# A graph-network kernel: messages of the last two aggregations in two float32r parts instead of three bf16 parts, with the cast of the counts shared by ScalarE and VectorE

## The chip, the cores and the metric

One core of a Trainium2 chip. The metric is the device time in microseconds (us) of one launch; lower is better. The chip multiplies on TensorE (PE in the profile's rows, PEld for its weight loads), and works element by element on VectorE (DVE), ScalarE (ACT) and GpSimd (POOL). SyncE (SP) issues most of the DMAs.

## What is computed

Four graph layers over 1875 nodes with 256 features and 60000 edges, each followed by a residual add and a layer norm. The change is in the third layer, which applies this convolution twice, with the same edges both times:

```python
def _sage_conv(x, src, dst, W_proj, b_proj, W_l, b_l, W_r):
    xp = jax.nn.relu(x @ W_proj + b_proj)
    msg_sum = jax.ops.segment_sum(xp[src], dst, num_segments=n)
    cnt = jax.ops.segment_sum(jnp.ones_like(dst, dtype=x.dtype), dst, num_segments=n)
    aggr = msg_sum / jnp.maximum(cnt, 1.0)[:, None]
    out = aggr @ W_l + b_l + x @ W_r
    norm = jnp.linalg.norm(out, axis=-1, keepdims=True)
    return out / jnp.maximum(norm, EPS)
```

`msg_sum` is what this text calls an aggregation: for each destination node, the sum of the rows `xp` of its sources.

## The kernel before, in words

**The counts.** In its long first part the kernel walks over the edges and builds the array `ADJ`: for each source node and each destination node the number of edges between them, as 16-bit integers. A partition holds one source of each tile of 128; the free dimension runs over 1888 destinations (`NW`) and, innermost, over 15 tiles of sources (`SH`, the same number as `NT`). One "chunk" of counts is what one tile of sources needs: 1888 elements, read at a stride of 15 elements.

**An aggregation** (`aggregate`, lines 1739 to 1757) is then a dense product. For each of the 15 chunks TensorE multiplies the messages of a source tile (128 by 256, the stationary operand, in two halves of 128 features) with the chunk (the moving operand, four pieces of 472 columns, `CW`), and adds in all eight PSUM banks. The messages are float32 values; to keep their precision they are held as a sum of three bf16 parts (hi, mid, lo), so a chunk costs 3 x 2 x 4 = 24 matmuls. The chunk is float16, which holds the small counts exactly. There are two chunk buffers: `chunk(at, c % 2, wide)`. ScalarE casts chunk c (`cast2`, lines 719 to 723, called from `messages2`) once TensorE has used chunk c - 2 (semaphore `chunk_used`), and TensorE waits for it (`chunk_ready`). Chunks 0 and 1 are cast early (`early_cast`): for the first convolution in the stage of the layer before, for the second during the output stage of the first. Two loops exist of everything, for small and for large counts (`wide`); with these inputs the small-count one runs. In the second layer there is a similar aggregation over 30 chunks (`CH1`), which the change leaves as it is.

**Messages.** Before an aggregation, `project` (line 1800) makes each tile of `x @ W_proj + b_proj` in one of four banks: one bf16 matmul for the bias and two float32 matmuls. ScalarE writes the relu of it as bf16 (`message`, line 678: hi). VectorE computes the rest from the bank: `rest` (line 1268), three dependent instructions: the remainder (line 1274), its bf16 cast (line 1275, mid), and the difference (line 1276, lo), after which `p_ev` lets TensorE use the bank again. TensorE starts the aggregation when all 15 tiles are through (line 1827).

**After an aggregation** VectorE and ScalarE copy the eight banks out (`agg_evac`, lines 1297 and 715). The output stage follows: for each of 15 tiles, float32 matmuls with `W_l` (line 1836) and `W_r` (line 1839), and the scaling, the norm and the relu on VectorE and ScalarE. In the first convolution the result is transposed on TensorE (line 1696) for the second.

**The order of the work** is written by hand, engine by engine. Every engine runs the loop `for u in range(2)` over the two convolutions: TensorE at line 1823, ScalarE at 753 (as v), VectorE at 1358. In the second one VectorE also runs `attention_columns` (line 1345): eight instructions on the weights of the fourth layer (lines 1350 and 1351). They stand between the last message and the copy of the banks. They wait for three DMAs (`ld_wt3`) that SyncE issues when the output stage of the first convolution is through TensorE.

Of the kernel before, what the change touches and what calls it, by code (L numbers as in the profile page):

```python
# [21 lines left out]
F32 = mybir.dt.float32  # L22
F16 = mybir.dt.float16
BF16 = mybir.dt.bfloat16
I32 = mybir.dt.int32
SP, DVE, PE = mybir.EngineType.SP, mybir.EngineType.DVE, mybir.EngineType.PE
U16 = mybir.dt.uint16
# [6 lines left out]
D = 256  # L34
P = 128
# [132 lines left out]
def build(nc, rec, x, xT, edge0, w0, a0l, a0r, cols, hrow, wrel, brow, wih, w1, w2, w3, b3, wp1, bp1, wl1, bl1, wr1, wp2, bp2, wl2, bl2, wr2,  # L168
          wt3, a3l, a3r, out):
    ctx = ExitStack()  # L170
    with ctx:
# [8 lines left out]
        sorted_t = nc.dram_tensor("sorted_records", (EP, 4), I32).ap()  # L180
        al_t = nc.dram_tensor("al_table", (NP, H), F32).ap()

        AR = sb("arena", [P, A_END], F32)
        ADJ = sb("adjacency", [P, R2, NW * SH], U16)
        ident = sb("ident", [P, P], F32)
# [119 lines left out]
        def parts(i):  # L305
            return [MT[i].bitcast(BF16)[:, D * q:D * (q + 1)] for q in range(3)]

        WIDE = [AR[:, A_B1 + D * i:A_B1 + D * (i + 1)] for i in range(R2 * NT)]

        def chunk(at, k, wide):  # L310

            if wide:
                return AR[:, at[1] + k * NW:at[1] + (k + 1) * NW]
            return AR[:, at[0] + k * NW // 2:at[0] + (k + 1) * NW // 2].bitcast(F16)
# [27 lines left out]
            feat_ev diag_done bc_mm sel_free collected cmp_done ws_mm selr_ready djr_mm sel_ready fld_mm fld_ev steps_done a_oh a_mm a_ev a_add  # L342
            pool_link lane_mm lane_ev flags_in flags_mm tail_ready tail_mm cin_ready cin_mm exp_ready exp_done
            alpha_ready als_mm als_ev r_oh r_wgt r_mm ld_hb ld_x ld_bc ld_wt1 ht_ready ht_add
            var_ready std_ready ln_done xt_mm xt_eva xt_evd h_mm h_ev m_mm m_ev chunk_ready chunk_used agg_eva
            agg_evd gate_mm gate_ev c_ready tc_ready hn_ready x1_mm x1_ev x2_mm x2_ev x3_mm x3_add ld_b2 ld_wt2 ld_wt3
            p_mm p_ev hi_ready cnt_red cnt_mm big_mm o_mm o_ready nrm_done h_ready pool_gate vl3_done t_mm t_ev t_st key_mm
            key_ev er_st er_ld erw_ready kc_ev oht er_mm er_red et_mm et_ev selt sc_mm flag_cmp flag_mm
# [213 lines left out]
        def _(act):  # L562
# [112 lines left out]
                    xt_evac(0, q - 1)  # L675
            xt_evac(0, 3)

            def message(n, bank, wide):

                dst = WIDE[n % (R2 * NT)] if wide else parts(n % (R2 * NT))[0]  # L680
                a.activation(dst, PS[bank][:, 0:D], ACT.Relu).then_inc(s["hi_ready"], 1)

            def messages1(wide):
# [35 lines left out]
            def cast2(v, c, wide):  # L719
                if c >= 2:  # L720
                    act.wait_ge(s["chunk_used"], (R2 + v) * SH + c - 1)
                a.activation(chunk(CH2, c % 2, wide), ADJ[:, 0, :].rearrange("p (n s) -> p n s", s=SH)[:, :, c],  # L722
                             ACT.Copy).then_inc(s["chunk_ready"], 1)

            def early_cast(v, c):
# [27 lines left out]
            for v in range(2):  # L753
                def messages2(wide):
                    for t in range(NT):
                        act.wait_ge(s["p_mm"], NT * v + t + 1)
                        message(t, t % 4, wide)
                    for c in range(2, SH):
                        cast2(v, c, wide)

                with act.If(large < 1):
                    messages2(False)
                with act.If(large >= 1):
                    messages2(True)
                agg_evac(B2T, (R2 + 1 + v) * SH)
                if v == 0:
                    early_cast(1, 0)
                    early_cast(1, 1)
                for q, (t0, t1) in enumerate(GROUPS):
                    act.wait_ge(s["o_ready"], NT * v + t1)  # L770
                    a.activation(RS[:, t0:t1], RS[:, t0:t1], ACT.Sqrt).then_inc(s["nrm_done"], 1)
                    if v == 0 and q:
                        xt_evac(2, q - 1)
                    if v == 1:
                        ln_sqrt(7 + q, t0, t1)
                    if v == 1 and q >= 2:
                        xt_evac(3, q - 2)
                if v == 0:
                    xt_evac(2, 3)
# [14 lines left out]
        def _(dve):  # L794
# [473 lines left out]
            def rest(n, slot, bank, done, before):  # L1268
# [6 lines left out]
                link(v.tensor_copy(mid, REM))  # L1275
                v.tensor_tensor(lo, REM, mid, ALU.subtract).then_inc(done, 1)  # L1276

            def no_rest(n, done):

                dve.wait_ge(s["hi_ready"], n + 1)  # L1280
                dve.sem_inc(s["dve_link"], 2)
                dve.sem_inc(done, 1)
# [62 lines left out]
            def attention_columns():  # L1345

                dve.wait_ge(s["ld_wt3"], 48)
                for lr in range(2):
                    for k in range(2):
# [5 lines left out]
                        else:  # L1355
                            link(ins)

            for u in range(2):
                with dve.If(large < 1):
                    for t in range(NT):  # L1360
                        rest(R2 * NT + u * NT + t, t, t % 4, s["p_ev"], u * NT + t)
                chain[0] -= 2 * NT
                with dve.If(large >= 1):
                    for t in range(NT):
                        no_rest(R2 * NT + u * NT + t, s["p_ev"])
                chain[0] += 2 * NT
                if u == 1:
                    attention_columns()
                agg_evac(B2T, base + (u + 1) * SH)
                for q, (t0, t1) in enumerate(GROUPS):  # L1370
                    for t in range(t0, t1):
                        dve.wait_ge(s["o_mm"], NT * u + t + 1)
                        link(v.tensor_scalar(B1[:, t, :], PS[t % 4][:, 0:D], RC[:, t:t + 1], None, ALU.mult))
                        link(v.tensor_tensor(B1[:, t, :], B1[:, t, :], PS[t % 4][:, D:2 * D], ALU.add))
                        v.tensor_tensor_reduce(out=REM, in0=B1[:, t, :], in1=B1[:, t, :], scale=1.0, scalar=0.0,
                                               op0=ALU.mult, op1=ALU.add, accum_out=RS[:, t:t + 1]).then_inc(s["o_ready"], 1)
                    if u == 1 and q:
                        normalise(6 + q, *GROUPS[q - 1])
                    dve.wait_ge(s["nrm_done"], 4 * u + q + 1)
                    link(v.tensor_scalar(RS[:, t0:t1], RS[:, t0:t1], 1e-12, None, ALU.max))  # L1380
                    link(v.reciprocal(RS[:, t0:t1], RS[:, t0:t1]))
                    for t in range(t0, t1):
                        if u == 0:
                            ins = v.tensor_scalar(B1[:, t, :], B1[:, t, :], RS[:, t:t + 1], 0.0, ALU.mult, ALU.max)
                        else:
                            ins = v.scalar_tensor_tensor(X[:, t, :], B1[:, t, :], RS[:, t:t + 1], X[:, t, :], ALU.mult, ALU.add)
                    if u == 0:
                        ins.then_inc(s["h_ready"], 1)
                        if q:
                            xt_evac(2, q - 1)  # L1390
                    else:
                        link(ins)
                        link(stats(t0, t1))
                        variance(t0, t1)
                        if q >= 2:
                            xt_evac(3, q - 2)
                if u == 0:
                    xt_evac(2, 3)
# [44 lines left out]
        def _(pe):  # L1443
# [295 lines left out]
            def aggregate(at, n, first):  # L1739


                def products(wide):
                    for c in range(n):
                        pe.wait_ge(s["chunk_ready"], first + c + 1)
                        ch = chunk(at, c % 2, wide)
                        ms = [WIDE[c]] if wide else parts(c)
                        for q, m in enumerate(ms):
                            for fo in range(2):
                                for j in range(4):
# [161 lines left out]
```

## Time and profile before

| | us |
|---|---|
| three runs of the kernel | 1827.79, 1826.61, 1823.5 |
| median | 1826.61 |
| span of the profiled execution, first to last instruction | 1946.7 |
| PE, DVE, ACT busy in it | 1461.8, 1153.3, 786.8 |
| first aggregation of the third layer, in the trace | 1599.1 to 1671.0 |
| second one | 1735.1 to 1809.8 |

For the profiled execution only its span is known, and it stands 120.1 us above the median of the runs that were timed without a profile. In the rows, `L1750` is line 1750 of the kernel before; a line such as "1599.13 71.87 PE L1750 ... x360" gives the start of a group of instructions, its length and how many they are. The count of matmuls for a float32 operand is twice that in the code: each is recorded as two instructions. A granted clock (PEclk) of 1.00 is TensorE's full 2.4 GHz; its lower level is 1.2 GHz.

### The profile page before, as it was taken

To read this page: it belongs to the slowest core of one execution; us is meant where nothing else is said; L and a number is where in the kernel's file an instruction comes from. 1 tells how busy PE (TensorE), PEld (TensorE's weight loads), DVE (VectorE), ACT (ScalarE), POOL (GpSimd) and SP (SyncE) were. 2 spreads that over 40 slices of the span, in tenths; PEclk is the share of its full clock that TensorE was granted. 3 is DMA by queue.
4 is the path that set the end of the run, shared out by engine and by line. 5 is a ranking of instruction groups with operands and counts; after the bars stand their busy time and mean duration, and the time that the engine had idled before them with its cause. 6 is when DMAs were issued, how large, how long until landed. Compare 5 with 4: busy or idle time off the path is not lost.

```text
span 1946.7 us, 22362 instructions
## 1 busy us (share of the span) xinstructions
PE 1461.8 (75%) x5398; PEld 733.7 (38%) x5398; DVE 1153.3 (59%) x3024; ACT 786.8 (40%) x1243; POOL 531.3 (27%) x517
## 2 busy tenths in 40 slices
PE   5894765577666766666359999798999889989930
PEld 3342433231111111111237777554445444644620
DVE  5412432239888988898999999852181460450636
ACT  1331332237666766676200000035774527327121
POOL 0105555556757666775000000000000000000023
PEclk9996555575555555555559999899999989999975
DMA  3535455554545455554129888300000010000022
GB/s 149 166 141 170 143 164 166 173 162 142 177 150 177 150 166 170 173 172 151 44 84 307 270 271 269 96 1 24 1 1 1 0 33 1 1 11 1 1 61 63
DMA packets 84509, 223.94 MB, mean 115 GB/s; under 512 B 18456, under 2 KB 27588, under 8 KB 83908
## 3 DMA queue, kind: packets, MB, share of 16 engines
q1 hardware_dynamic: 60452, 158.01, 23.4%
q0 software_dynamic: 23968, 64.77, 12.6%
q8 instruction: 53, 0.87, 0.2%
q14 instruction: 36, 0.29, 0.0%
HBM read 140.09 MB, written 82.63 MB: 114 GB/s over the span
## 4 chain that ended last, share of the span: by engine, by line
PE 38%; DVE 15%; issue 6%; DVEq 2%; ACT 1%; DMA 1%; POOL 0%; another core or an unknown queue 0%; SPq 0%; POOLq 0%
PE bank L1750 15%; PE bank L1687 11%; PE bank L1770 2%; DVE arena L1126 2%; DVE arena L1084 2%; PE bank L1734 2%; DVE adjacency L1091 2%; PE bank L1709 1%; DVE arena L1085 1%; PE bank L1839 1%; PE bank L1836 1%; PE bank L1816 1%; DVE arena L1276 1%; DVE arena L1274 1%; DVE arena L1172 1%
## 5 line engine op out<-in xcount | busy, mean ns | idle before, releaser
L547 POOL DMA_INDIRECT arena<-feat_table,arena x469 | 494.5, 1054 | 365.6 <-issue 231.4
L1626 PE MATMUL bank<-arena 128*128 128x480 f16 x586 | 337.2, 577 | 165.9 <-DVE arena L1085 96.7
L629 ACT ACTIVATE arena<-bank 128x480 uint16<-128x480 f32 x586 | 332.6, 572 | 164.4 <-PE bank L1626 109.4
L1750 PE MATMUL bank<-arena 128*128 128x472 f16 x1440 | 291.4, 366 | 10.5 <-DVE arena L1276 6.5
L555 POOL DMA_INDIRECT arena<-al_table,edge_ends x15 | 14.3, 956 | 964.7 <-DMA al_table<-arena 960.4
L1091 DVE TENSOR_TENSOR adjacency<-adjacency,arena 128x480 uint16 x586 | 234.3, 400 | 38.8 <-issue 22.8
L1687 PE MATMUL bank<-arena 128*128 x966 | 229.5, 392 | 0.8 <-issue 0.3
L1626 PEld LDWEIGHTS bank<-arena 128*128 128x128 f16 x586 | 60.9, 104 | 442.4 <-issue 219.9
L1750 PEld LDWEIGHTS bank<-arena 128*128 128x128 bf16 x1440 | 141.8, 99 | 160.2 <-issue 12.4
L1085 DVE TENSOR_SCALAR arena<-iota,arena 128x480 f16<-128x480 f16 x586 | 199.0, 340 | 0.0
L1687 PEld LDWEIGHTS bank<-arena 128*128 128x128 f32 x966 | 174.0, 190 | 56.6 <-issue 35.3
L1182 DVE TENSOR_TENSOR arena<-arena 128x1024 f32<-128x1024 f32 x118 | 140.3, 1213 | 16.9 <-DMA arena<-edge_rows 15.2
L1084 DVE TENSOR_SCALAR arena<-iota,arena 128x128 f16<-128x128 f16 x586 | 145.4, 248 | 4.1 <-ACT adjacency L593 4.1
L722 ACT ACTIVATE arena<-adjacency 128x1888 f16<-128x1888 uint16 x30 | 108.8, 3633 | 45.9 <-PE bank L1750 45.9
L703 ACT ACTIVATE arena<-adjacency 128x1888 f16<-128x1888 uint16 x30 | 109.0, 3636 | 33.7 <-PE bank L1750 33.7
L1589 PE MATMUL bank<-arena 128*128 x588 | 75.9, 187 | 53.3 <-issue 47.7
L1546 PE MATMUL bank<-arena 128*128 128x512 f32 x240 | 111.4, 620 | 5.9 <-ACT arena L578 3.0
L605 ACT ACTIVATE arena<-bank 128x512 f16<-128x512 f32 x64 | 35.3, 597 | 173.6 <-remote 81.1
L1575 PE MATMUL bank<-adjacency,ident 128*128 128x512 f16 x128 | 67.4, 617 | 47.1 <-DVE arena L1041 35.5
L661 ACT ACT_TABLE_LOAD x2 | 2.6, 1283 | 239.8 <-DVE ln_mean_var L1228 239.8
L1297 DVE COPY arena<-bank 128x472 f32<-128x472 f32 x12 | 7.0, 642 | 143.4 <-PE bank L1750 143.3
L1589 PEld LDWEIGHTS bank<-arena 128*128 128x128 f16 x588 | 58.6, 105 | 86.4 <-issue 74.7
(289 smaller groups left out, 1544.6 us busy)
## 6 DMA issues: line engine op xcount, KB each, us to landing
arena<-edge_rows SPq DMA_DIRECT2D x117, 520.0 KB, 4.7
edge_rows<-arena SPq DMA_DIRECT2D x67, 520.0 KB
edge_rows<-arena SPq DMA_DIRECT2D x67, 390.0 KB
feat_table<-arena SPq DMA_DIRECT2D x60, 260.0 KB, 2.1
arena<-feat_table,arena POOLq DMA_INDIRECT x469
arena<-in_w SPq DMA_DIRECT2D x1, 2048.0 KB, 10.1
arena<-in_xT SPq DMA_DIRECT2D x1, 1920.0 KB, 18.3
arena<-in_x SPq DMA_DIRECT2D x1, 1792.0 KB
```

What stands on the lines that cost most here:

```text
L547: g.indirect_dma_start(out=PLACE[k][:, t - lo, :], out_offset=None, in_=feat_t, in_offset=bass.IndirectOffsetOnAxis(ap=IE[:, t:t + 1], axi ...
L629: a.activation(EV[st % AS].rearrange("p r k -> p (r k)"), PS[4 + st % 4][:, 0:R2 * KW], ACT.Copy)\
L703: a.activation(chunk(CH1, c % 2, wide), ADJ[:, r, :].rearrange("p (n s) -> p n s", s=SH)[:, :, sh], ACT.Copy).then_inc(s["chunk_ready"], 1)
L1084: v.tensor_scalar(OHS[st % AS], iota128[:, :], lo, None, ALU.is_equal)
L1085: v.tensor_scalar(OHK[st % AS], iota480[:, :], key, None, ALU.is_equal).then_inc(s["a_oh"], 1)
L1091: v.tensor_tensor(dst, dst, EV[st % AS], ALU.add).then_inc(s["a_add"], 1)
L1182: v.tensor_tensor(rows, rows, al, ALU.mult).then_inc(s["r_wgt"], 1)
L1546: ins = mm(PS[c][:, :], XT0[:, k, P * t:P * (t + 1)], W0[:, k, 512 * c:512 * (c + 1)], start=(k == 0), stop=(k == 1))
L1589: ins = mm(PS[4 + g % 2][:, 3 * H * k:3 * H * (k + 1)], KO[g % 3][:, lo:lo + P], ERW[:, bass.ds(offs[k], 3 * H)], start=True, stop=True)
L1626: mm(PS[4 + st % 4][:, 0:R2 * KW], OHS[st % AS], OHK[st % AS], start=True, stop=True).then_inc(s["a_mm"], 1)
L1687: mm(BANKS[:, bass.ds(out_at, D)], OHR[:, (st // RG) % ORING, P * (st % RG):P * (st % RG + 1)], FBf[:, bass.ds(places[st % RK] >> 12, D)], ...
L1750: ins = mm(PS[4 * fo + j][:, 0:CW], m[:, P * fo:P * (fo + 1)], ch[:, CW * j:CW * (j + 1)], start=(c == 0 and q == 0), stop=(c == n - 1 and ...
```

## The change

Only the two aggregations of the third layer change (`CH2`).

- A message is held as two parts of type float32r, hi and lo, in a new view of the same memory (`halves`, `HALVES`). ScalarE writes hi; VectorE writes lo in one instruction (`low_half`) instead of the three of `rest`. 
- A chunk is float32r too (`COUNTS`). A chunk costs 2 x 2 x 4 = 16 matmuls instead of 24. Both operands of each are now float32r.
- From chunk 2 on ScalarE casts the first 944 destinations of a chunk and VectorE the other 944 (`second_halves`), after a wait of its own for `chunk_used`; a new semaphore `chunk_half` adds a second wait to TensorE's. ScalarE still casts chunks 0 and 1 whole.
- In the second convolution `attention_columns` moves on VectorE ahead of the messages.

```diff
--- before.py
+++ after.py
@@ -22,6 +22,7 @@
 F32 = mybir.dt.float32
 F16 = mybir.dt.float16
 BF16 = mybir.dt.bfloat16
+F32R = mybir.dt.float32r
 I32 = mybir.dt.int32
 SP, DVE, PE = mybir.EngineType.SP, mybir.EngineType.DVE, mybir.EngineType.PE
 U16 = mybir.dt.uint16
@@ -180,6 +181,7 @@
         sorted_t = nc.dram_tensor("sorted_records", (EP, 4), I32).ap()
         al_t = nc.dram_tensor("al_table", (NP, H), F32).ap()
 
+        a_at = -(-nc.sbuf_base // 32) * 32
         AR = sb("arena", [P, A_END], F32)
         ADJ = sb("adjacency", [P, R2, NW * SH], U16)
         ident = sb("ident", [P, P], F32)
@@ -305,10 +307,18 @@
         def parts(i):
             return [MT[i].bitcast(BF16)[:, D * q:D * (q + 1)] for q in range(3)]
 
+        HALVES = nc.alloc_sbuf_tensor_at("message_halves", [P, 2 * NT * D], F32R, offset=a_at + 4 * A_B1)
+        COUNTS = nc.alloc_sbuf_tensor_at("count_chunks", [P, 2 * NW], F32R, offset=a_at + 4 * A_CH)
+
+        def halves(i):
+            return [HALVES[:, D * (2 * i + q):D * (2 * i + q + 1)] for q in range(2)]
+
         WIDE = [AR[:, A_B1 + D * i:A_B1 + D * (i + 1)] for i in range(R2 * NT)]
 
         def chunk(at, k, wide):
 
+            if at == CH2 and not wide:
+                return COUNTS[:, k * NW:(k + 1) * NW]
             if wide:
                 return AR[:, at[1] + k * NW:at[1] + (k + 1) * NW]
             return AR[:, at[0] + k * NW // 2:at[0] + (k + 1) * NW // 2].bitcast(F16)
@@ -342,7 +352,7 @@
             feat_ev diag_done bc_mm sel_free collected cmp_done ws_mm selr_ready djr_mm sel_ready fld_mm fld_ev steps_done a_oh a_mm a_ev a_add
             pool_link lane_mm lane_ev flags_in flags_mm tail_ready tail_mm cin_ready cin_mm exp_ready exp_done
             alpha_ready als_mm als_ev r_oh r_wgt r_mm ld_hb ld_x ld_bc ld_wt1 ht_ready ht_add
-            var_ready std_ready ln_done xt_mm xt_eva xt_evd h_mm h_ev m_mm m_ev chunk_ready chunk_used agg_eva
+            var_ready std_ready ln_done xt_mm xt_eva xt_evd h_mm h_ev m_mm m_ev chunk_ready chunk_half chunk_used agg_eva
             agg_evd gate_mm gate_ev c_ready tc_ready hn_ready x1_mm x1_ev x2_mm x2_ev x3_mm x3_add ld_b2 ld_wt2 ld_wt3
             p_mm p_ev hi_ready cnt_red cnt_mm big_mm o_mm o_ready nrm_done h_ready pool_gate vl3_done t_mm t_ev t_st key_mm
             key_ev er_st er_ld erw_ready kc_ev oht er_mm er_red et_mm et_ev selt sc_mm flag_cmp flag_mm
@@ -675,9 +685,9 @@
                     xt_evac(0, q - 1)
             xt_evac(0, 3)
 
-            def message(n, bank, wide):
-
-                dst = WIDE[n % (R2 * NT)] if wide else parts(n % (R2 * NT))[0]
+            def message(n, bank, wide, exact=False):
+
+                dst = WIDE[n % (R2 * NT)] if wide else halves(n)[0] if exact else parts(n % (R2 * NT))[0]
                 a.activation(dst, PS[bank][:, 0:D], ACT.Relu).then_inc(s["hi_ready"], 1)
 
             def messages1(wide):
@@ -719,7 +729,8 @@
             def cast2(v, c, wide):
                 if c >= 2:
                     act.wait_ge(s["chunk_used"], (R2 + v) * SH + c - 1)
-                a.activation(chunk(CH2, c % 2, wide), ADJ[:, 0, :].rearrange("p (n s) -> p n s", s=SH)[:, :, c],
+                n = NW if c < 2 else NW // 2
+                a.activation(chunk(CH2, c % 2, wide)[:, 0:n], ADJ[:, 0, :].rearrange("p (n s) -> p n s", s=SH)[:, 0:n, c],
                              ACT.Copy).then_inc(s["chunk_ready"], 1)
 
             def early_cast(v, c):
@@ -754,7 +765,7 @@
                 def messages2(wide):
                     for t in range(NT):
                         act.wait_ge(s["p_mm"], NT * v + t + 1)
-                        message(t, t % 4, wide)
+                        message(t, t % 4, wide, True)
                     for c in range(2, SH):
                         cast2(v, c, wide)
 
@@ -1274,6 +1285,12 @@
                 link(v.scalar_tensor_tensor(REM, PS[bank][:, 0:D], 0.0, hi, ALU.max, ALU.subtract))
                 link(v.tensor_copy(mid, REM))
                 v.tensor_tensor(lo, REM, mid, ALU.subtract).then_inc(done, 1)
+
+            def low_half(n, slot, bank, done):
+
+                hi, lo = halves(slot)
+                dve.wait_ge(s["hi_ready"], n + 1)
+                v.scalar_tensor_tensor(lo, PS[bank][:, 0:D], 0.0, hi, ALU.max, ALU.subtract).then_inc(done, 1)
 
             def no_rest(n, done):
 
@@ -1355,17 +1372,24 @@
                         else:
                             link(ins)
 
+            def second_halves(u, wide):
+                for c in range(2, SH):
+                    dve.wait_ge(s["chunk_used"], (R2 + u) * SH + c - 1)
+                    v.tensor_copy(chunk(CH2, c % 2, wide)[:, NW // 2:NW], ADJ[:, 0, :].rearrange("p (n s) -> p n s", s=SH)[:, NW // 2:NW, c])\
+                     .then_inc(s["chunk_half"], 1)
+
             for u in range(2):
+                if u == 1:
+                    attention_columns()
                 with dve.If(large < 1):
                     for t in range(NT):
-                        rest(R2 * NT + u * NT + t, t, t % 4, s["p_ev"], u * NT + t)
-                chain[0] -= 2 * NT
+                        low_half(R2 * NT + u * NT + t, t, t % 4, s["p_ev"])
+                    second_halves(u, False)
                 with dve.If(large >= 1):
                     for t in range(NT):
-                        no_rest(R2 * NT + u * NT + t, s["p_ev"])
-                chain[0] += 2 * NT
-                if u == 1:
-                    attention_columns()
+                        dve.wait_ge(s["hi_ready"], R2 * NT + u * NT + t + 1)
+                        dve.sem_inc(s["p_ev"], 1)
+                    second_halves(u, True)
                 agg_evac(B2T, base + (u + 1) * SH)
                 for q, (t0, t1) in enumerate(GROUPS):
                     for t in range(t0, t1):
@@ -1742,8 +1766,10 @@
                 def products(wide):
                     for c in range(n):
                         pe.wait_ge(s["chunk_ready"], first + c + 1)
+                        if at == CH2 and c >= 2:
+                            pe.wait_ge(s["chunk_half"], (first // SH - R2) * (SH - 2) + c - 1)
                         ch = chunk(at, c % 2, wide)
-                        ms = [WIDE[c]] if wide else parts(c)
+                        ms = [WIDE[c]] if wide else halves(c) if at == CH2 else parts(c)
                         for q, m in enumerate(ms):
                             for fo in range(2):
                                 for j in range(4):
```

## Rows read from the trace of the kernel before

**Rows 1.** Windows: length, busy time by engine, granted clock, DMA share, GB/s.
```profile
1599.10:1671.00 71.90, 71.87 (x360) 35.14 (x360) 0.00 (x0) 47.19 (x13) 0.00 (x0) 1.00 0.00 1
...
1735.10:1809.80 74.70, 74.59 (x360) 35.89 (x360) 3.19 (x9) 47.23 (x14) 0.00 (x0) 0.96 0.00 1
```

**Rows 2.** Timeline, first aggregation: start, length, instruction, idle before.
```profile
1604.12 3.63 ACT L722 ACTIVATE arena<-adjacency 128x1888 f16<-128x1888 uint16 x1 [7.05 <-PE bank L1750]
1608.90 3.62 ACT L722 ACTIVATE arena<-adjacency 128x1888 f16<-128x1888 uint16 x1 [1.15 <-PE bank L1750]
...
1599.13 71.87 PE L1750 MATMUL bank<-arena 128*128 128x472 f16 x360 [2.48 <-DVE arena L1276]
```

**Rows 3.** Chain of waits in the first output stage: start, length, piece.
```profile
1675.88 0.86 PE bank L1836 x4
...
1690.83 0.87 PE bank L1696 x8
```

**Rows 4.** Groups by form: busy us, mean ns; float32 weight loads.
```profile
L1836 PEld LDWEIGHTS bank<-arena 128*128 128x128 f32 x120 | 22.8, 193 | 9.2 <-DVE arena L1298 5.9 <-DVE ln_rstd L1375 0.4
```

**Rows 5.** Groups by form: a ScalarE copy to float16; VectorE reads.
```profile
L605 ACT ACTIVATE arena<-bank 128x512 f16<-128x512 f32 x64 | 35.3, 597 | 173.6 <-remote 81.1 <-PE bank L1577 50.9 <-PE bank L1575 28.7
...
L1302 DVE TENSOR_REDUCE arena<-adjacency 128x1888 f32<-128x28320 uint16 x1 | 29.7, 29653 | 0.0
...
L1422 DVE TENSOR_REDUCE arena<-arena 128x64 f32<-128x256 f32 x15 | 7.8, 576 | 0.1
```

**Rows 6.** Timeline: end of the first convolution's messages.
```profile
1595.52 1.13 PE L1807 MATMUL bank<-arena 128*128 128x256 f32 x4
...
1596.69 0.38 ACT L681 ACTIVATE arena<-bank 128x256 bf16<-128x256 f32 x1 [0.89 <-PE bank L1807]
...
1598.53 0.43 DVE L1276 TENSOR_TENSOR arena<-arena 128x256 bf16<-128x256 f32 x1
```

**Rows 7.** Timeline: the second convolution's messages.
```profile
1710.50 1.13 PE L1807 MATMUL bank<-arena 128*128 128x256 f32 x4
...
1711.77 1.13 PE L1807 MATMUL bank<-arena 128*128 128x256 f32 x4
...
1714.01 0.82 PE L1696 MATMUL bank<-ident,arena 128*128 128x128 f32 x6
...
1714.87 0.56 DVE L1242 COPY arena<-bank 128x384 f32<-128x384 f32 x1 [3.74 <-PE bank L1696]
...
1716.61 0.28 PE L1805 MATMUL bank<-arena,ones 3*128 3x256 bf16 x1 [1.78 <-DVE arena L1276]
...
1728.45 0.28 PE L1805 MATMUL bank<-arena,ones 3*128 3x256 bf16 x1
...
1729.77 0.28 PE L1805 MATMUL bank<-arena,ones 3*128 3x256 bf16 x1
...
1729.98 1.13 PE L1807 MATMUL bank<-arena 128*128 128x256 f32 x4
...
1734.90 0.42 DVE L1350 TENSOR_TENSOR arena<-arena 128x256 f32<-128x256 f32 x1
```

**Rows 8.** Timeline: the last instruction of attention_columns; the last DMA issued for it.
```profile
1738.09 0.42 DVE L1351 TENSOR_REDUCE arena<-arena 128x4 f32<-128x256 f32 x1
...
1708.47 0.43 SPq L472 DMA_DIRECT2D arena<-in_a3r  x1
```

**Rows 9.** DMA view: us from issue to landing.
```profile
arena<-in_a3r SPq DMA_DIRECT2D x1, 128.0 KB, 3.1
```

**Rows 10.** Timeline of TensorE after three pauses.
```profile
1735.15 74.59 PE L1750 MATMUL bank<-arena 128*128 128x472 f16 x360 [4.04 <-DVE arena L1276]
...
1740.23 0.15 PEld L1750 LDWEIGHTS bank<-arena 128*128 128x128 bf16 x1 [0.24 <-issue]
...
1673.48 1.13 PE L1836 MATMUL bank<-arena 128*128 128x256 f32 x4 [2.48 <-DVE arena L1298]
...
1812.22 1.97 PE L1836 MATMUL bank<-arena 128*128 128x256 f32 x4 [2.48 <-DVE arena L1298]
```

## The prediction

> **What bounds the kernel now.** The windows by stage come first [rows 1]. They show two stretches of 71.9 and 74.7 us in which TensorE is busy without a break on 360 matmuls each, with no DMA and hardly any work on VectorE; ScalarE is busy 47 us of each. These are the two aggregations that the change touches: 146.6 us. The timeline of the first shows who leads [rows 2]: 71.87 us for 360 matmuls, 199.6 ns each. ScalarE's casts start every 4.78 us (1604.12, 1608.90), which is 24 x 199.2 ns, one chunk of TensorE; a cast takes 3.63 us, and ScalarE then waits 1.15 us for TensorE. So TensorE sets the pace, with ScalarE not far behind. With 16 matmuls a chunk would be 3.19 us, shorter than an undivided cast.
>
> **The price of a float32r matmul** is the one unknown that matters: no row has one. A float32 matmul of 256 columns is two records, and four records take 0.86 us [rows 3], so one matmul takes 430 ns or 1.68 ns per column, four times the 0.42 ns per column of the float16 ones (199.2 / 472). Lower bound: float32r goes as float16 does, 199 ns for 472 columns. Upper bound: it goes as float32 does, 472 x 1.68 = 793 ns. Between them lie a float32 record (half a matmul, 0.84 ns per column, so 397 ns) and a float16 matmul with an uncovered weight load (199 + 109 = 308 ns, where 109 ns is the spacing of float32 transposes of 128 columns [rows 3], each with its own load). I take 199 ns. Two products of parts with half the bits each are what the two parts of the change stand for, and four such products are the factor of 4 in the row; a single product of 4-byte operands is then a quarter of it. That argues for one pass, but it doesn't prove it, as a factor of 2 x 2 with two cycles per column fits the same rows.
>
> The Trainium skill, page "FP8 and Floating Point Precision", section "TensorE Precision Notes", says that true FP32 makes four passes through the array and that a reduced mode reads 4-byte values and truncates them; by the four passes a single pass is the 199 ns above, and the trace's factor of 4 agrees. It gives no rate for float32r.
>
> Weight loads: in bf16 a load is recorded at 98 ns (35.14 us for 360) [rows 1], in float32 at 193 ns [rows 4]. The bf16 ones vanish behind their matmuls, and four float32 records of 215 ns each carry a load each and run at 0.84 ns per column, so those are covered too. A matmul of 199 ns is longer than the 109 ns spacing; I cost the load at nothing. If that cover is gone it is the 308 ns above.
>
> **The parts of the change.**
> - *Aggregations.* 16 x 199.2 = 3.19 us a chunk, 15 chunks 47.8 us in place of 71.87: -24.1 us each, -48.1 us in all.
> - *Casts.* A relu of 256 columns takes ScalarE 0.38 us [rows 6] and 512 columns to float16 0.597 us [rows 5]: 0.83 ns per element and about 0.17 us fixed. The cast of 1888 strided elements costs 3.63 us [rows 2], so 1.83 ns each; half a chunk is 944 x 1.83 + 0.17 = 1.9 us. VectorE's half is between 944 x 1.05 = 1.0 us, by a plain pass over the same array (29.65 us for 28320 elements), and 944 x 576 / 256 = 2.1 us, by a short strided read [rows 5]; I take 1.7 us, nearer the strided one. Both start when a buffer is free, 0.2 us after its chunk (1599.13 + 4.78 to 1604.12) [rows 2], and have 3.19 us until TensorE needs it. Even 2.1 us leaves 0.9 us. Zero on the path. Undivided, the cast would make 3.63 + 0.2 us the pace. The second wait of TensorE is on a semaphore long raised: between 0 and 0.1 us at each of 26 chunks, I take 0, and 2.6 us is the upper end. VectorE's waits hold up nothing: behind them stands only the copy of the banks, which needs the last chunk anyhow.
> - *First convolution's messages.* TensorE sets the pace, 1.27 us a tile (1710.50 to 1711.77) [rows 7]. Its last matmul ends at 1596.65; ScalarE writes hi until 1597.07; VectorE is behind and ends at 1598.96, and TensorE starts at 1599.13, 0.17 us later [rows 2, 6]. With one instruction of 0.42 us in place of three, lo is done at 1597.53 and TensorE starts at 1597.70: -1.4 us.
> - *Second convolution's messages.* Now VectorE is the pace, 1.32 us a tile (1728.45 to 1729.77). After: VectorE is free at 1715.43 [rows 7]. attention_columns goes first: 3.61 us, from 1734.90 to 1738.51 [rows 7, 8]. Its data are there: issued at 1708.47, landed 3.1 us later [rows 8, 9]. Until then the four banks stay full: TensorE, which in the trace went on at 1716.61 after 1.78 us, goes on at about 1719.57 (1715.43 + 3.61, 0.1 of latency, 0.42 for lo): +3.0 us. Then 10 tiles at 1.27 us and the last one's 1.34 (1729.77 to 1731.11) end at 1733.6, and hi, lo and latency (0.04 + 0.38 + 0.04 + 0.42 + 0.17) put the aggregation at 1734.65 instead of 1735.15 [rows 10]: -0.5 us. The move gives back most of what the shorter lo saves there.
> - *TensorE's clock.* The second aggregation began after a pause of 4.04 us, with its first 14 matmuls at 393 ns (the 1.2 GHz level) until 1740.6, and cost 74.59 us instead of 71.87: 2.7 us [rows 10]. After the change this pause is 1.05 us and the stretch stays at 2.4 GHz; but a pause of 4.7 us (1714.83 to 1719.57) arises before project tile 4, and a drop falls there, at a like price. Net zero. Pauses of 2.48 us went both ways: the clock held at 1673.48 (1.13 us for four records) and fell at 1812.22 (1.97) [rows 10]. With 2.7 us as the most that one drop costs, the ends are -5.4 (neither the new drop nor the one at 1812) and +2.7 (one more, after the first aggregation).
> - *hi and early casts.* ScalarE's 512 columns to float16 take the 0.597 us of [rows 5] at the same pace as above, so an output of another width is costed at nothing; nor does the first layer's work or any DMA change.
>
> Sum: -48.1 - 1.4 - 0.5 = **-50.0 us**. Against the profiled execution's span of 1946.7 that is 1896.7. That execution is 120.1 us above the median of 1826.61; the matmuls' 199 ns is 472 columns at 2.4 GHz, so the saving should be the same outside the profile: **1776.5 us**.
>
> **Rivals.**
> 1. *Weight loads uncovered* (5 in 100). 16 x 308 ns is 4.93 us a chunk, 73.9 us an aggregation; against 71.87, +4.1 us for both, less the 1.9 of the messages: +2.2, about 1829. Against it: float32 records hide their loads. The break-even lies at 299 ns a matmul (24/16 x 199.2). The Trainium skill, page "TensorE: Matmul & The Clock Gate", Part 3, says that a weight load overlaps a running matmul only when it goes to another row group. By that rule the bf16 matmuls of this trace, all on 128 rows, would be 199 + 98 ns apart; they are 199.6 apart, so the trace speaks against it.
> 2. *Slower: two cycles per column* (8 in 100). The moving operand is 4 bytes wide, and both the float32 record and the transpose (109 ns for 128 columns) show 0.85 ns per column [rows 3]. It decides wherever a matmul takes over 299 ns, in both aggregations. Then 397 ns a matmul, 6.35 us a chunk, 95.3 us an aggregation: +23.4 each, in all +45, about 1871. For it: every single record of 4-byte operands in the trace goes at this pace. Against it: the factor of 4 would need only two products.
> 3. *No cheaper than float32* (5 in 100): 793 ns, 190 us an aggregation, +237 less 1.9, about 2062. The type would then be a name only.
> 4. *The cast sets the pace* (3 in 100): if the halves don't shrink in time as they do in size, 3.63 + 0.2 = 3.83 us over 13 chunks, +8.3 us an aggregation, about 1793, still faster.
>
> **How the numbers follow.** My forecast has 79 in 100. Its own range: the clock down to -5.4, the timed runs' spread of about 2 us, so 1769; upwards 2.7 of clock, 2.6 of waits, 2 of spread give 1784, and every 10 ns by which a matmul misses 199 costs 4.8 us (480 of them), so 1790 allows 13 ns more; rival 4's 1793 lies just outside. The range is 1769 to 1790. A measurement of this kernel can tell about 0.2%, 3.7 us, from no change. Faster: the forecast, rival 4 and a load only partly uncovered, 0.84. Same: most of rival 1, 0.03. Slower: rivals 2 and 3, 0.13.
>
> **What would show it.** In the profile of the changed kernel: 240 matmuls an aggregation in about 48 us at 199 ns with a clock of 1.00; ScalarE's half casts of 1.9 us every 3.19 us, VectorE's of 1.0 to 2.1 beside them, both waiting for TensorE; the first aggregation starting 1 us after the last project matmul; TensorE waiting 4.7 us for VectorE before tile 4 of the second convolution, with matmuls at half pace behind it. A matmul of 300 ns or more proves me wrong, as does a TensorE that waits for a cast.

## The result and the profile after

| | median, us | ratio to before, 95% interval |
|---|---|---|
| before (4 runs) | 1826.96 | |
| changed (4 runs, 1781.72 to 1784.86) | 1784.26 | 0.977 [0.9753, 0.9787] |
| forecast | 1776.5 (1769 to 1790) | |

The change saves 42.7 us; 50.0 were forecast. The profiled execution of the changed kernel took 1781.72 us, with a span of 1780.0, so it needs no correction of the kind that the one before did.

The windows of the changed kernel, for the first aggregation, the messages of the second convolution, and the second aggregation (columns as in [rows 1]):

```profile
1478.70:1530.40 51.70, 51.69 (x240) 45.00 (x240) 15.05 (x13) 27.76 (x13) 0.00 (x0) 1.00 0.00 1
1568.80:1597.50 28.70, 22.60 (x87) 13.61 (x85) 12.76 (x34) 6.52 (x18) 0.00 (x0) 0.88 0.07 19
1597.50:1649.30 51.80, 51.71 (x240) 45.00 (x240) 15.12 (x13) 27.73 (x13) 0.00 (x0) 1.00 0.00 1
```

240 matmuls take 51.70 us where 360 took 71.87 [rows 1, 2]. That is 215.4 ns each, at the full granted clock, and not 199. TensorE is busy for 51.69 of the 51.70 us: nothing that the change added makes it wait. The groups by form of the changed kernel, and its timeline in the first aggregation, show the casts:

```profile
L733 ACT ACTIVATE count_chunks<-adjacency 128x944 fp32r<-128x944 uint16 x26 | 55.5, 2134 | 39.8 <-PE bank L1776 39.8
...
L1378 DVE CAST count_chunks<-adjacency 128x944 fp32r<-128x944 uint16 x26 | 30.2, 1161 | 62.2 <-PE bank L1776 62.2
```
```profile
1482.42 2.13 ACT L733 ACTIVATE count_chunks<-adjacency 128x944 fp32r<-128x944 uint16 x1 [4.34 <-PE bank L1776]
1485.85 2.13 ACT L733 ACTIVATE count_chunks<-adjacency 128x944 fp32r<-128x944 uint16 x1 [1.29 <-PE bank L1776]
...
1482.43 1.15 DVE L1378 CAST count_chunks<-adjacency 128x944 fp32r<-128x944 uint16 x1 [3.89 <-PE bank L1776]
1485.85 1.20 DVE L1378 CAST count_chunks<-adjacency 128x944 fp32r<-128x944 uint16 x1 [2.27 <-PE bank L1776]
```

Both halves start together every 3.43 us (1482.42, 1485.85), which is 16 x 214.4 ns, and both engines then wait for TensorE, ScalarE 1.29 us and VectorE 2.27 us. (The 215.4 above is a mean over a whole aggregation, with its start and the full length of its last matmul; the same two figures of the kernel before are 199.6 and 199.2.) The reader can check the cover here: the idle time ahead of each cast, less the 0.2 us from the end of a chunk to the start of a cast, is the slack. The casts beside the matmuls don't slow them. The last pair starts when the third chunk from the end is through, at 1523.59, and is done at 1525.71; the copy of the banks, released by the last chunk, starts at 1530.45. That is 6.86 us for two chunks, 3.43 each like all others, though no cast runs in the last 4.7 us.

The timeline of the second convolution's messages, which answers to [rows 7, 8 and 10]:

```profile
1575.02 0.82 PE L1720 MATMUL bank<-ident,arena 128*128 128x128 f32 x6
...
1576.35 0.41 DVE L1367 TENSOR_TENSOR arena<-arena 128x256 f32<-128x256 f32 x1
...
1579.53 0.42 DVE L1368 TENSOR_REDUCE arena<-arena 128x4 f32<-128x256 f32 x1
1579.87 1.41 DVE L1293 SCALAR_TENSOR_TENSOR message_halves<-bank,message_halves 128x256 fp32r<-128x256 f32 x4
...
1580.34 0.39 PE L1831 MATMUL bank<-arena,ones 3*128 3x256 bf16 x1 [4.51 <-DVE message_halves L1293]
...
1580.66 2.08 PE L1833 MATMUL bank<-arena 128*128 128x256 f32 x4
...
1582.99 2.08 PE L1833 MATMUL bank<-arena 128*128 128x256 f32 x4
...
1585.24 1.13 PE L1833 MATMUL bank<-arena 128*128 128x256 f32 x4
...
1597.59 6.69 PE L1776 MATMUL bank<-count_chunks,message_halves 128*128 128x472 f32 x30 [1.05 <-DVE message_halves L1293]
```

attention_columns (1576.35 to 1579.95) now stands ahead of VectorE's first lo. TensorE sits idle for 4.51 us and then runs two tiles at half pace: 2.08 us for four records instead of 1.13. From there it is never held up again, and the aggregation starts after a pause of 1.05 us with its clock at 2.4 GHz.

### The profile page after: what moved, and what is told of

Its sections match the earlier page's. It is cut to its first block, busy times and chain, and to the rows that moved or that the text cites. A ratio compares the mean times of both kernels' runs of the same rounds, so it can differ in the third digit from the quotient of the medians.

```text
span 1780.0 us, 21845 instructions
## 1 busy us (share of the span) xinstructions
PE 1422.1 (80%) x5158; PEld 758.0 (43%) x5158; DVE 1154.4 (65%) x2990; ACT 749.8 (42%) x1243; POOL 546.0 (31%) x517
## 4 chain that ended last, share of the span: by engine, by line
PE 43%; DVE 20%; issue 14%; POOL 6%; DMA 2%; ACT 2%; DVEq 2%; SPq 0%; POOLq 0%
PE bank L1776 14%; PE bank L1711 13%; POOL arena L557 6%; DVE arena L1095 4%; DVE arena L1096 3%; DVE adjacency L1102 3%; PE bank L1796 2%; DVE arena L1137 2%; PE bank L1833 2%; PE bank L1758 2%; PE bank L1733 2%; DMA arena<-feat_table,arena 1%; PE bank L1865 1%; DVEq L372 1%; PE bank L1862 1%
## 5 line engine op out<-in xcount | busy, mean ns | idle before, releaser
L557 POOL DMA_INDIRECT arena<-feat_table,arena x469 | 508.8, 1085 | 240.1 <-issue 227.9
L1096 DVE TENSOR_SCALAR arena<-iota,arena 128x480 f16<-128x480 f16 x586 | 199.2, 340 | 0.0
L1776 PE MATMUL bank<-arena 128*128 128x472 f16 x720 | 146.2, 367 | 3.9 <-ACT arena L713 3.9
L713 ACT ACTIVATE arena<-adjacency 128x1888 f16<-128x1888 uint16 x30 | 109.0, 3638 | 34.9 <-PE bank L1776 34.9
L1776 PE MATMUL bank<-count_chunks,message_halves 128*128 128x472 f32 x480 | 103.4, 377 | 2.1 <-DVE message_halves L1293 2.1
L1776 PEld LDWEIGHTS bank<-arena 128*128 128x128 bf16 x720 | 71.1, 99 | 79.3 <-ACT arena L713 4.7
L1776 PEld LDWEIGHTS bank<-count_chunks,message_halves 128*128 128x128 f32 x480 | 90.0, 188 | 15.5 <-issue 2.9
L733 ACT ACTIVATE count_chunks<-adjacency 128x944 fp32r<-128x944 uint16 (+1 forms) x30 | 69.9, 2335 | 39.8 <-PE bank L1776 39.8
L1200 DVE TENSOR_TENSOR arena<-iota,arena 128x1024 f32<-128x1024 f16 (+1 forms) x61 | 73.8, 1210 | 7.0 <-PE bank L1711 6.9
```

The source lines that it names most:

```text
L557: g.indirect_dma_start(out=PLACE[k][:, t - lo, :], out_offset=None, in_=feat_t, in_offset=bass.IndirectOffsetOnAxis(ap=IE[:, t:t + 1], axi ...
L713: a.activation(chunk(CH1, c % 2, wide), ADJ[:, r, :].rearrange("p (n s) -> p n s", s=SH)[:, :, sh], ACT.Copy).then_inc(s["chunk_ready"], 1)
L1096: v.tensor_scalar(OHK[st % AS], iota480[:, :], key, None, ALU.is_equal).then_inc(s["a_oh"], 1)
L1776: ins = mm(PS[4 * fo + j][:, 0:CW], m[:, P * fo:P * (fo + 1)], ch[:, CW * j:CW * (j + 1)], start=(c == 0 and q == 0), stop=(c == n - 1 and ...
```

## The experiments

Two things were open. Where do the 16 ns per matmul come from (215.4 against the 199.2 of the forecast), worth 480 x 16.2 = 7.8 us, a little more than the whole shortfall of 7.3? And what did the move of attention_columns cost? One theory was that float32r itself is dearer than 16-bit operands, by a floor, a fixed amount or a rate; the rival was that something around the matmuls (the second wait, casts running beside them) slows them down. Line numbers below are those of each kernel, so `L1776` can be L1772, L1777 or L1778.

**The changed kernel again.** No edit.

> The changed kernel as it is, as the measure for the others on this chip. Both theories of the shortfall (the saving was 42.7 us where 50.0 were forecast) expect the time of the first comparison, 1782 to 1785 us, and 215 ns per float32r matmul in both aggregations.

Measured: 1782.94 us, ratio 0.9765 [0.974, 0.9789], and 51.71 us for each aggregation. As expected.

**The move undone.**

```diff
 for u in range(2):
-    if u == 1:
-        attention_columns()
     with dve.If(large < 1):
 ...
         second_halves(u, True)
+    if u == 1:
+        attention_columns()
     agg_evac(B2T, base + (u + 1) * SH)
```

> attention_columns goes back behind the messages and VectorE's half casts of the second convolution; all else as in the changed kernel. My reading of the trace (the move costs TensorE's pause of 4.51 us before tile 4 and the drop of its clock after it): the pause shrinks to about 1.1 us (-3.4), two project tiles no longer run at half clock (-2.1), and the eight instructions hide in VectorE's free time of the aggregation: 5 to 6 us less than the changed kernel. The rival (the pause is filled by other waits, or the eight instructions now delay a half cast or the copy of the banks): within 1 us of it, or up to 4 us more.

Measured: 1777.94 us, ratio 0.9729 [0.9703, 0.9756], 5.0 us below the changed kernel run beside it. The timeline of this kernel, at the same place:

```profile
1572.04 0.82 PE L1720 MATMUL bank<-ident,arena 128*128 128x128 f32 x6
...
1573.37 0.75 DVE L1293 SCALAR_TENSOR_TENSOR message_halves<-bank,message_halves 128x256 fp32r<-128x256 f32 x2
...
1573.84 0.28 PE L1831 MATMUL bank<-arena,ones 3*128 3x256 bf16 x1 [0.99 <-DVE message_halves L1293]
```

The pause is 0.99 us instead of 4.51. The chain of waits gives the two aggregations of this kernel:

```profile
1475.73 51.71 PE bank L1776 x240
1588.94 51.71 PE bank L1776 x240
```

Between the end of the first and the start of the second lie 1588.94 - 1475.73 - 51.71 = 61.50 us; in the changed kernel it is 1597.59 - 1478.71 - 51.71 = 67.17. Of the 5.7 us, 3.5 are the pause and the rest, 2.1, is about what two project tiles lose at half clock (2.33 instead of 1.27 us each). The rival is refuted: the eight instructions found room in VectorE's free time and ended 2.2 us before the banks were ready to copy, and neither that copy nor a half cast was late. Run again on another occasion, with the same edit:

> The undone move once more, on the same chip as the next two. In the traces it took the stretch between the aggregations from 67.2 to 61.5 us. Expected about 1778 us, 5 us below the changed kernel's 1783.

Measured: 1777.29 us, ratio 0.9734 [0.9706, 0.9762]. The intervals of the ratio still overlap those of the changed kernel, so the timed runs alone wouldn't settle 5 us; the stretch between the aggregations does. It was 61.5 us in all four traces without the move (the 16-bit parts with it undone included), and between 65.0 and 70.5 in the eight traces with it. In each of these eight the pause was 4.51 us; two tiles behind it ran at or near half pace, in two of the eight traces four tiles.

**Two 16-bit parts instead of two float32r parts.**

```diff
 def halves(i):
-    return [HALVES[:, D * (2 * i + q):D * (2 * i + q + 1)] for q in range(2)]
+    return [MT[i].bitcast(BF16)[:, 0:D], MT[i].bitcast(F16)[:, D:2 * D]]
 ...
-            if at == CH2 and not wide:
-                return COUNTS[:, k * NW:(k + 1) * NW]
```

> As the changed kernel, but the two parts of a message are a bf16 hi and a float16 lo, and the counts are float16 again; lo keeps 11 bits, so a message has some 19 to 20 bits instead of 24. Still 16 matmuls a chunk and the shared cast. If the type float32r costs 215 instead of 199 ns a matmul: 199 ns, 47.8 us an aggregation instead of 51.7, 7 to 8 us less than the changed kernel. If the 15 ns come from something else that the change brought (the second wait, two engines reading the counts beside TensorE): 215 ns remain and the time stays.

Measured: 1771.75 us, ratio 0.9699 [0.967, 0.9728], 11.2 us below the changed kernel. Both aggregations in this kernel's chain of waits, and its casts in the groups by form:

```profile
1474.45 47.98 PE bank L1772 x240
1589.47 47.98 PE bank L1772 x240
```
```profile
L729 ACT ACTIVATE arena<-adjacency 128x944 f16<-128x944 uint16 x26 | 50.0, 1923 | 38.4 <-PE bank L1772 38.4
...
L1374 DVE CAST arena<-adjacency 128x944 f16<-128x944 uint16 x26 | 26.7, 1025 | 59.0 <-PE bank L1772 59.0
```

199.9 ns a matmul with the same waits and the same two engines casting. So the 15.5 ns between 199.9 and 215.4 belong to the type; the 0.7 ns left of the 16.2 come from setting a mean over an aggregation, ends included, against the 199.2 of the forecast, which was a spacing without them. Both operands changed their type here, so the run doesn't tell which of them costs it. The two aggregations explain 7.5 of the 11.2 us. Another 3.1 lie ahead of the first one: from the last matmul of the layer before to the first aggregation this trace took 27.6 us and the changed kernel beside it 30.7, with its first three project tiles at half pace.

**Narrower matmuls of the lo part.**

```diff
-    ins = mm(PS[4 * fo + j][:, 0:CW], m[:, P * fo:P * (fo + 1)], ch[:, CW * j:CW * (j + 1)],
+    ins = mm(PS[4 * fo + j][:, 0:w], m[:, P * fo:P * (fo + 1)], ch[:, CW * j:CW * j + w],
```

Here w is 472 for hi; for lo it is 384 in the first aggregation and 256 in the second, and 240 and 128 in the second experiment of this kind.

> As the changed kernel, but the matmuls of the lo part take only the first 384 (first aggregation) and 256 (second) of each 472 columns; the products of lo with the others are left out. Theory A, the 4-byte weight load is a floor under a matmul: about 214 ns at 384 and at 256 columns as at 472. Theory B, a fixed 15 ns on top of the columns: 178 and 124 ns. Theory C, every column of a float32r operand takes 0.455 ns instead of 0.42: 175 and 116 ns.

> As the run with narrow lo matmuls, but with 240 (first aggregation) and 128 columns (second) of each 472. There 384 and 256 columns came to 176.7 and 116.8 ns, in proportion to the columns (0.456 to 0.460 ns each), with nothing fixed on top. If that holds below 256 columns: 109 and 58 ns. If the weight load (the float32 transposes of 128 columns are 109 ns apart) is a floor: 109 and 109 ns. If short float32r matmuls lose the single pass: four times the columns, over 400 and over 200 ns.

The aggregations in the chain of waits, with 384 and 256 columns:

```profile
1482.21 47.06 PE bank L1777 x240
1595.88 39.88 PE bank L1777 x240
```

And with 240 and 128 columns:

```profile
1480.09 39.27 PE bank L1777 x240
1589.75 39.37 PE bank L1777 x240
```

Half of each 240 matmuls have 472 columns and take 120 x 0.2154 = 25.85 us; the rest divided by 120 is the narrow one's time:

| columns | ns per matmul | ns per column |
|---|---|---|
| 472 | 215.4 | 0.456 |
| 384 | 176.8 | 0.460 |
| 256 | 116.9 | 0.457 |
| 240 | 111.8 | 0.466 |
| 128 | 112.7 | 0.880 |

Down to 256 columns the time is in proportion to the columns, 0.456 to 0.460 ns each against 0.422 for the 16-bit operands; theory C holds, and a floor (A) or a fixed amount (B) at these widths does not. From 240 to 128 columns a matmul gets no shorter: a floor of about 112 ns, near the 109 ns between two float32 transposes [rows 3], as the second of the three expectations had it. The 128 columns show it; at 240 the rate alone would give 109 ns. ScalarE still waited for TensorE there (18.8 us over 26 casts), so the casts didn't set it; I put it down to the weight load, which no run changed by itself. The loss of the single pass below 256 columns, the third possibility, did not show. The timed single runs were 1769.23 and 1759.15 us.

**One cast instead of two halves.**

```diff
-                n = NW if c < 2 else NW // 2
+                n = NW
```

With it go `second_halves` and TensorE's wait for `chunk_half`.

> As the changed kernel, but ScalarE casts each chunk whole and VectorE casts nothing. My account: the whole cast takes 3.64 us, with 0.25 us until it starts 3.9 us a chunk against TensorE's 3.43, so ScalarE sets the pace for 13 chunks: +0.45 x 13 = +5.9 us an aggregation, about 12 us more than the changed kernel. Rival (the casts are hidden anyway, as in the kernel before): the same time.

Measured: 1788.65 us, ratio 0.9819 [0.9765, 0.9872], 5.7 us above the changed kernel of the earlier comparison, where 12 were expected. The intervals overlap, so the timed runs don't separate the two kernels; the traces do. The timelines of TensorE and ScalarE in the second and first aggregation:

```profile
1597.66 7.13 PE L1772 MATMUL bank<-count_chunks,message_halves 128*128 128x472 f32 x32 [1.05 <-DVE message_halves L1293]
1605.36 7.55 PE L1772 MATMUL bank<-count_chunks,message_halves 128*128 128x472 f32 x32 [0.57 <-ACT count_chunks L733]
...
1651.64 3.69 PE L1772 MATMUL bank<-count_chunks,message_halves 128*128 128x472 f32 x16 [0.21 <-ACT count_chunks L733]
```
```profile
1478.69 50.19 ACT L733 ACTIVATE count_chunks<-adjacency 128x1888 fp32r<-128x1888 uint16 x13 [4.34 <-PE bank L1772]
```

13 casts run back to back in 50.19 us, 3.86 each, and the releaser of TensorE's idle time is now the cast. The second aggregation takes 1651.64 + 3.69 - 1597.66 = 57.7 us: +6.0, as expected, but not for the reason given. The expectation was 3.64 us for a cast and 0.25 until it starts; the trace shows no wait between the casts, and each takes longer, 3.92 us as recorded (the records overlap a little). The same instruction takes 3.64 to 3.65 us outside the aggregations. VectorE does nothing in this stretch, so it is not what slows ScalarE; what is left is TensorE's float32r aggregation beside it, since in the kernel before, beside 16-bit matmuls, the cast to float16 took 3.63.

The pace-setting is shown. That the whole run is only some 5 us slower comes from other stages of the two traces, in which TensorE ran less at half pace. From the last matmul of the layer before (it ends at 1447.91) to the first aggregation (1474.98) it took 27.1 us, against 30.7 in the changed kernel, which ran its first three project tiles at half pace there. Between the aggregations it took 65.0 us against 67.2, and behind the second 128.8 against 130.7. That is 7.7 us less in all, against 11.9 more in the aggregations, and the spans differ by 4.1. Why the clock fell less often here stays open.

**All later casts on VectorE.**

```diff
+                if c >= 2:
+                    act.sem_inc(s["chunk_ready"], 1)
+                    return
 ...
-                    v.tensor_copy(chunk(CH2, c % 2, wide)[:, NW // 2:NW], ADJ[:, 0, :].rearrange(...)[:, NW // 2:NW, c])\
+                    v.tensor_copy(chunk(CH2, c % 2, wide), ADJ[:, 0, :].rearrange(...)[:, :, c])\
```

> As the changed kernel, but VectorE casts chunks 2 to 14 whole and ScalarE none of them. Two accounts of why a half cast to float32r takes 2.13 us on ScalarE and 1.16 on VectorE, where one to float16 took 1.92 and 1.03: if the two engines are in each other's way, VectorE alone needs 2 x 1.03 minus one fixed part, 1.9 to 2.0 us, for a whole chunk; if the type is dearer to write, 2.2 to 2.3. Either way it is hidden behind TensorE's 3.43 us and the time stays as in the changed kernel, within 2 us.

Measured: 1784.35 us, a single run, within 2 us of the changed kernel. The cast in the groups by form:

```profile
L1380 DVE CAST count_chunks<-adjacency 128x1888 fp32r<-128x1888 uint16 x26 | 54.6, 2100 | 39.7 <-PE bank L1778 39.7
```

A whole chunk takes VectorE 2.10 us, less than ScalarE needs for half of one beside it, and less than 2 x 1.16. It falls between the two accounts (1.9 to 2.0, and 2.2 to 2.3), so for VectorE the runs don't settle how much of the dearer half cast is the type and how much the company. For ScalarE the type alone costs nothing: outside the aggregations a whole chunk takes 3.64 us to float32r and 3.63 to float16. So its dearer half cast (2.13 against 1.92 us) comes from what runs beside it, as the dearer whole one does in the experiment before this. The runs do settle that VectorE alone would do, and that the split was needed only to relieve ScalarE.

**Both gains together:** the 16-bit parts and the move undone, two edits shown above.

> Both edits together: a bf16 hi and a float16 lo (less precise than the two float32r parts) with float16 counts, and attention_columns back behind the messages and half casts. If both gains are real and independent: 7.4 us from 480 matmuls at 199 to 200 instead of 215 ns, and 5.5 us from the pause and the clock, so about 1770 where the changed kernel takes 1783, below both kernels. If the clock of TensorE drops elsewhere instead, 3 us of it are missing.

Measured: 1769.84 us, ratio 0.969 [0.9654, 0.9727]. That was only 1.9 us below the 16-bit parts alone, so both were run again on one chip:

> The 16-bit parts without the undone move, once more. Expected 1772 to 1776 us: 7.5 us below the changed kernel by the matmuls; the 11 us of the first comparison held some luck with the clock in the stage before.

> Both edits once more. If they add, 3.5 to 5.6 us less than the 16-bit parts alone on this chip; in the first comparison it was only 1.9, with the clock low for 3 us before the first aggregation in the trace. If the gain of the undone move is eaten up here, no difference.

Measured: 1776.41 us, 0.9727 [0.9696, 0.9757], for the 16-bit parts alone, and 1767.89 us, 0.9685 [0.9657, 0.9713], for both. The difference is 8.5 us this time; in the traces it is 5.5 us of the stretch between the aggregations in the first pair (67.0 and 61.5) and 9.0 in the second (70.5 and 61.5), so the gain is real and its size depends on the clock. In the first pair the stretch ahead of the first aggregation took 3.2 us more with both edits than with one (30.8 and 27.6), again with three project tiles at half pace, and that hid part of it. The combined version beats both kernels: the whole of its interval lies below that of the changed kernel. It carries less precise messages, 19 to 20 bits by the widths of its two formats (no run here measures the error); the undone move alone leaves the arithmetic as it is and is worth 5 us.

**The kernel before, a second trace.**

> The kernel before once more, for a second trace: the first one's span was 120 us above the timed runs. Expected: a span near 1825 us with the same 71.9 to 74.7 us per aggregation, so that the 120 us lie before the third layer.

Measured: 1830.52 us, span 1828.8. TensorE's timeline of its two aggregations:

```profile
1482.70 73.55 PE L1750 MATMUL bank<-arena 128*128 128x472 f16 x360 [2.31 <-DVE arena L1276]
1624.30 71.87 PE L1750 MATMUL bank<-arena 128*128 128x472 f16 x360 [2.15 <-DVE arena L1276]
```

The last matmul of the second layer ends at 1449.01 here and ended at 1569.84 in the first trace: 120.8 us, more than the whole difference of the two spans (117.9), lie ahead of what the change touches. The clock's part also moved: here the first aggregation lost 1.7 us to it and the second none; in the first trace it was the second, with 2.7.

## Why the prediction was right, and where its sum was off

- *TensorE sets the pace of the aggregations, and fewer matmuls shorten them.* Right: 240 matmuls without a gap.
- *"I take 199 ns."* This is the term that was mis-sized. A float32r matmul of 472 columns takes 215.4 ns. The aggregations saved 20.2 us each instead of 24.1: 40.3 in place of 48.1, and 7.8 us of shortfall against the 7.3 by which the time missed. The price of about a quarter of float32's was right, and rivals 1 to 3 (uncovered loads, two cycles per column, no cheaper than float32) are refuted. The forecast was the lower bound of its own range of prices, so any error in it could only lengthen the run. The range allowed a matmul 13 ns more and it took 16; the time stayed inside because the allowances for clock, waits and spread were not used up. With 215.4 ns the sum gives 1776.5 + 7.8 = 1784.3, against 1784.26 measured. That is closer than the clock's scatter from run to run allows to foresee, and so partly luck.
- *Weight loads at nothing.* Right at 472 columns. They are recorded at 188 ns each (45.00 us for 240), yet 256 columns ran at 116.9 ns. The floor of 112 ns below that is near the 109 ns spacing by which I priced an uncovered load.
- *Casts at nothing.* Right. I had 1.9 us for ScalarE and 1.7 for VectorE; it was 2.13 and 1.16. The strided read hardly costs VectorE anything: 1.11 ns per element for a whole chunk, near the plain pass's 1.05 [rows 5]. The pace of an undivided cast came out at 3.86 us against 3.83, but by luck: the sum was 3.63 and a wait of 0.2, and the trace has no wait and a cast of 3.9.
- *First convolution's messages, -1.4 us.* The pause ahead of the aggregation went from 2.48 us [rows 2], 2.31 in the second trace, to 1.05: right.
- *Second convolution's messages.* The pause of 4.7 us was forecast and 4.51 measured. The fall of the clock behind it was forecast as well; it came in all eight traces with the move, at 1.6 to 2.1 us for two tiles in six of them, but at some 4 us for four tiles in two of them, more than the 2.7 I had allowed. The net of -0.5 us can only be estimated: the stretch between the aggregations took 67.17 us, of which 2.1 are these two tiles and 1.6 slow matmuls just behind the first aggregation (47.45 us from there to the end of the pause, against 45.86 in the trace of one cast, which has none). That leaves 63.5, against 64.15 in the first trace of the kernel before: -0.7. The forecast added that the move gives back most of what the shorter lo saves there; the runs show that nothing was gained for it, and that undoing it costs nothing.
- *TensorE's clock, net zero.* Not testable to a few us: the stretch before the first aggregation alone took between 27.1 and 33.7 us over the traces, with zero to four project tiles at half pace and a wait for a DMA of 0.6 to 1.9 us in it. Such differences are why 5 us show better in a stage than in the run's time.

## What to carry to other kernels

When an operand's type changes, price its matmul by a rate of its own: here float32r took about a quarter of float32's time, but 8% more per column than 16-bit operands, and 480 matmuls made 7.5 us of it. When work is moved within an engine's program, ask who waits behind it: 3.6 us of VectorE's work that had been free beside an aggregation became a pause of 4.5 us for TensorE ahead of it, and the pause cost some 2 us more through the clock, in two traces 4. Where the timed runs scatter by as much as the effect, compare the stretch between two fixed points of the trace.

## What the runs showed of the hardware that I had not expected

- A float32r matmul streams at 0.456 to 0.460 ns per column at 256 to 472 columns, at a granted clock of 1.00, where bf16 with float16 takes 0.422 (199.2 ns) and a quarter of a float32 matmul 0.42 [rows 3]. What holds it back wasn't found; only a floor and a fixed amount are ruled out, and the waits and casts of the new scheme.
- From 240 to 128 columns such a matmul, with its own weight load, doesn't get shorter: 111.8 ns and 112.7.
- ScalarE takes 3.64 us to cast 1888 strided 16-bit integers to float32r, VectorE 2.10 us.
- Beside float32r matmuls ScalarE's cast to float32r slows, from 3.64 to 3.9 us with VectorE idle, while the matmuls keep their pace. Which part of TensorE's work does it was not tried.
